# Token layers of a language-model tower: maxima by one transfer into 24 rows, parts split from PSUM, new order table

## The chip, the cores and the metric

One core of a Trainium2 chip runs the whole kernel: five engines (TensorE, VectorE or DVE, ScalarE or ACT, GpSimd or POOL, SyncE or SP) with queues of their own, and 16 DMA engines. The metric is the device time of one execution in microseconds (us).

## The reference, cut to what matters

The reference is a tower of five stages over 8 x 256 tokens of width 128: a four-layer transformer encoder (the *token layers*), a landmark attention mixer, a mixture of experts over frequencies, an attention with eight wide heads and a grouped attention chosen per sequence. The change touches the token layers alone:

```
x = embed[src] + _pos_encoding(s, D)
for i in range(N):                      # N = 4 layers, H = 8 heads of DK = 16
    q = (x @ Wq[i] + bq[i]).reshape(b, s, H, DK).transpose(0, 2, 1, 3)
    k = (x @ Wk[i] + bk[i]).reshape(b, s, H, DK).transpose(0, 2, 1, 3)
    v = (x @ Wv[i] + bv[i]).reshape(b, s, H, DK).transpose(0, 2, 1, 3)
    scores = jnp.einsum('bhqd,bhkd->bhqk', q, k) * scale        # scale = DK ** -0.5
    attn = jax.nn.softmax(scores, axis=-1)
    o = jnp.einsum('bhqk,bhkd->bhqd', attn, v)
    o = o.transpose(0, 2, 1, 3).reshape(b, s, D) @ Wo[i] + bo[i]
    x = _layernorm(x + o, g1[i], be1[i])
    f = jax.nn.relu(x @ W1[i] + b1[i]) @ W2[i] + b2[i]
    x = _layernorm(x + f, g2[i], be2[i])
return _layernorm(x, gf, bf)
```

Eight sequences of 256 tokens are held as four pairs (PAIRS = 4) of two sequences, b = 0 and b = 1. Everything is fp32 in the reference.

## The kernel before, in words

**Number format.** The score products run in bf16 with fp32 accuracy: q and k are each split into three bf16 parts that sum to the fp32 value. `packed` (one tensor for queries, side 0, and one for keys, side 1) holds per head 96 rows (MROW = 96): six stacked pairs of a query part and a key part, 16 features each. A matmul over 96 rows gives the fp32-like score.

**Softmax.** The scores are computed twice. First (steps M, `banks<-t_packed 96*128`, L2320) with queries in the rows of the result, from which DVE takes the negated row maximum (steps m, L2510). The maxima are split into three bf16 parts (Mp, L2518 to L2521), turned by TensorE to 24 rows (three parts by eight heads; MT, L2329), copied to SBUF by ACT (mt, L2436), stored to DRAM by a DMA on ACT's queue (ms, L2443) and loaded by another (ml, L2448) into the three rows 96 to 98 of side 0 of `packed`, one row per part, head by head. Side 1 holds ones in these three rows, filled once at the setup by ACT (L2739) and DVE (L2695). Then the scores are computed again with keys in the rows (steps S, 99 rows, L2341), the maximum already subtracted, ACT takes the exponential (E, L2455), and TensorE multiplies with v (AV, L2355).

**Splitting q and k.** A projection (Aq, Ak, L2308) leaves 128x512 in one of two PSUM banks, `lin`. ACT copies it with scale and bias to fp32 in SBUF (fq, fk, into `qf`) and once more to bf16 (pq, pk, first part). POOL subtracts (rq, rk, L2576), ACT rounds the remainder to bf16 (yq, yk, L2429), POOL subtracts again (zq, zk, L2582). SP stores the three parts to DRAM (sq, sk, L2251) and loads them again in three transfers each (lq, lk, L2257), which regroup them by head: 1.5 MB per pair. A load waits for the landing of its store (`keys_stored`, `parts_stored`).

**The other steps.** V and Vc (value projection), O, T1, TR, T2, t2 (the heads' result, transposed and divided), C1 (output projection), C1d, C1p, X1 (layer norm: sums and statistics on DVE, reciprocal root and normalisation, 3.1 us, on POOL, L2600), C2 and C2c (transpose), C3 and H (first feed-forward product and relu), C4 (second), C4d, C4p, X2 (norm), C5 and C5c (transpose into `xT` for the next layer), N1a to N2b (residual, POOL), W (SP loads the next layer's weights and waits for them), WP (POOL reorders the projection weights), RB (POOL adds the first output bias to the residual).

**What sets the order.** The table `PLACES` gives each step of each engine a time relative to its pair, and `PERIOD` the distance from pair to pair. `places_of` sorts step times plus PERIOD x pair for all 16 pair-layers; the sorted list is the instruction order of that engine. The times act through this order alone; semaphores do the rest. A step is issued only when all before it on its engine are. SP's queue runs stores, loads and W in order too. The 17 steps in LIN_STEPS take the two `lin` banks by turns in PE's order, and one may begin only when the step two before it in that list has been read out (`read_out`).

## Time and profile before

| what | value |
|---|---|
| median of 3 runs | 1250.07 us (1244.36 to 1254.27) |
| profiled execution, its own time | 1243.97 us |
| its span, first to last instruction | 1242.2 us |
| TensorE matmul busy | 1015.9 us, 82% |
| DVE, ACT, POOL busy | 688.1, 615.6, 418.2 us |
| mean granted TensorE clock | 0.902 of full |

The profiled execution's time and its span differ by 1.8 us of start and end. It lies 6.1 us under the median of the runs. The token layers run from 32.7 us (first projection) to 563.9 us (last residual); before that is the setup with the gather of the embeddings. In a timeline row the first number is the start, the second the busy time. Matmuls overlap their neighbours' ends, so the distance from one start to the next says what a step takes.

### The profile page before, as it was taken

To read this page: it belongs to the slowest core of one execution; us is meant where nothing else is said; L and a number is where in the kernel's file an instruction comes from. 1 tells how busy PE (TensorE), PEld (TensorE's weight loads), DVE (VectorE), ACT (ScalarE), POOL (GpSimd) and SP (SyncE) were. 2 spreads that over 40 slices of the span, in tenths; PEclk is the share of its full clock that TensorE was granted. 3 is DMA by queue.
4 is the path that set the end of the run, shared out by engine and by line. 5 is a ranking of instruction groups with operands and counts; after the bars stand their busy time and mean duration, and the time that the engine had idled before them with its cause. 6 is when DMAs were issued, how large, how long until landed. Compare 5 with 4: busy or idle time off the path is not lost. (4 is left out here: it accounts for less than half of the span.)

```text
span 1242.2 us, 20645 instructions
## 1 busy us (share of the span) xinstructions
PE 1015.9 (82%) x7048; PEld 706.4 (57%) x7048; DVE 688.1 (55%) x1957; ACT 615.6 (50%) x1369; POOL 418.2 (34%) x460
## 2 busy tenths in 40 slices
PE   1358999998999998852797999996999999834787
PEld 1124655555565555431486577785788888822453
DVE  4156766776777766126455111125577777857663
ACT  3235666665666665424534523325455555441455
POOL 5323656665676665457302000014300000031110
PEclk9678999998999999885698899997999999955789
DMA  7343644443343342002000011000000000008440
GB/s 89 76 104 71 148 97 92 103 95 78 79 119 79 90 92 54 3 1 69 1 1 1 19 34 35 23 25 1 18 10 10 19 27 1 2 13 141 78 89 28
DMA packets 52392, 65.70 MB, mean 53 GB/s; under 512 B 9629, under 2 KB 45881, under 8 KB 49209
## 3 DMA queue, kind: packets, MB, share of 16 engines
q1 hardware_dynamic: 49256, 62.35, 22.1%
q0 software_dynamic: 512, 1.05, 1.3%
q10 hardware_dynamic: 2520, 0.99, 0.4%
q8 instruction: 58, 0.95, 0.3%
q14 instruction: 46, 0.37, 0.1%
HBM read 47.09 MB, written 17.27 MB: 52 GB/s over the span
## 5 line engine op out<-in xcount | busy, mean ns | idle before, releaser
L2510 DVE TENSOR_REDUCE t_nmax<-banks 128x2 f32<-128x512 f32 x256 | 167.6, 687 | 66.6 <-PE banks L2320 63.5
L2455 ACT ACTIVATE t_probs<-banks 128x512 f32<-128x512 f32 x256 | 149.8, 593 | 69.4 <-PE banks L2341 65.5
L2341 PE MATMUL banks<-t_packed 99*128 99x256 bf16 x512 | 102.3, 284 | 21.9 <-DMA t_packed<-t_max_parts 21.2
L2320 PE MATMUL banks<-t_packed 96*128 96x256 bf16 x512 | 99.9, 280 | 23.6 <-DMA t_packed<-t_qk_pairs 20.5
L2600 POOL TENSOR_SCALAR xhat<-t_rbuf,mv,rstd 128x128 f32<-128x128 f32 x128 | 100.1, 795 | 3.3
L2320 PEld LDWEIGHTS banks<-t_packed 96*128 96x128 bf16 x512 | 45.9, 99 | 85.4 <-issue 52.2
L2341 PEld LDWEIGHTS banks<-t_packed 99*128 99x128 bf16 x512 | 44.5, 100 | 75.0 <-issue 35.8
L2355 PE MATMUL banks<-t_probs,t_v 128*32 128x256 f32 x1024 | 85.6, 403 | 0.1
L1548 ACT ACTIVATE hid<-banks,b 128x512 f32<-128x512 f32 x64 | 43.5, 686 | 69.5 <-PE banks L1453 68.8
L1872 ACT ACTIVATE l_probs<-banks,l_shift 128x256 f32<-128x256 f32 x128 | 59.5, 472 | 30.8 <-DVE l_shift L1911 28.1
L707 POOL TENSOR_TENSOR n_rstd<-n_vareps,mhalf 128x4 f32<-128x4 f32 x4 | 4.0, 1006 | 208.0 <-DVE n_nmean L690 207.9
L1591 DVE SCALAR_TENSOR_TENSOR acc<-banks,gates,acc 128x128 f32<-128x128 f32 (+1 forms) x72 | 20.1, 343 | 96.7 <-PE banks L1473 96.7
L2396 PE MATMUL banks<-x1T,wff 128*128 128x512 f32 x128 | 69.6, 633 | 0.9 <-ACT x1T L2474 0.9
L1473 PE MATMUL banks<-w,hid 128*128 128x128 f32 (+1 forms) x576 | 68.6, 280 | 1.1 <-DVE acc L1405 0.8
L1827 PE MATMUL banks<-vp,l_pT 128*128 128x128 f32 x512 | 67.9, 276 | 0.0
L1827 PEld LDWEIGHTS banks<-vp,l_pT 128*128 128x128 f32 x512 | 63.3, 192 | 6.2 <-issue 6.2
L1473 PEld LDWEIGHTS banks<-w,hid 128*128 128x128 f32 (+1 forms) x576 | 64.6, 184 | 3.6 <-DVE acc L1405 0.9
L1805 PE MATMUL banks<-xT,l_tq 128*128 128x256 f32 x256 | 65.9, 380 | 0.0
L2590 POOL TENSOR_SCALAR vareps<-mv 128x4 f32<-128x4 f32 x32 | 7.5, 234 | 166.4 <-DVE mv L2553 166.4
L2545 DVE TENSOR_TENSOR t_rbuf<-banks,R 128x512 f32<-128x512 f32 x32 | 22.1, 692 | 72.4 <-PE banks L2402 65.2
L2402 PE MATMUL banks<-wff,hidden 128*128 128x128 f32 x512 | 60.0, 275 | 0.8 <-ACT hidden L2481 0.8
L1453 PE MATMUL banks<-hT,w 128*128 128x512 f32 x128 | 59.8, 622 | 0.0
(364 smaller groups left out, 2305.1 us busy)
## 6 DMA issues: line engine op xcount, KB each, us to landing
t_qk_pairs<-t_parts SPq DMA_DIRECT2D x32, 384.0 KB, 2.5
t_packed<-t_qk_pairs SPq DMA_DIRECT2D x32, 384.0 KB, 6.3
t_packed<-t_qk_pairs SPq DMA_DIRECT2D x32, 256.0 KB, 6.0
g_packed<-g_qk_parts SPq DMA_DIRECT2D x48, 128.0 KB, 4.2
t_packed<-t_qk_pairs SPq DMA_DIRECT2D x32, 128.0 KB, 6.7
w<-in_L_ffn_w SPq DMA_DIRECT2D x16, 256.0 KB, 2.6
g_qk_parts<-g_parts SPq DMA_DIRECT2D x8, 384.0 KB, 4.9
wff<-in_L_tok_W SPq DMA_DIRECT2D x8, 256.0 KB, 7.7
```

Source lines behind the costliest of these rows:

```text
L1453: pe.matmul(banks[:, n % 4, :], w1[:, j, c * P:(c + 1) * P], hT[:, k * PW:(k + 1) * PW], start=True, stop=True).then_inc(sem["up_ready"], 1)
L1473: ins = pe.matmul(banks[0:rows, 4 + n % 2, k * P:(k + 1) * P], hid[:, j, c, i * P:i * P + rows], w2[:, j, c, :], start=(c == 0), stop=(c = ...
L1805: ins = pe.matmul(sc[:, n % 3, qt * S:(qt + 1) * S], tq[:, h % 2, c:c + P], m.xT[:, b * S:(b + 1) * S], start=True, stop=True)
L1827: ins = pe.matmul(av[:, n % 2, qt * D:(qt + 1) * D], pT[:, n % 2, kt, qt * P:(qt + 1) * P], vp[:, h % 2, 2 * b + kt, 0:D], start=(kt == 0) ...
L2320: ins = pe.matmul(m.mbank[:, n % 3, i * S:(i + 1) * S], m.packed[0:MROW, 0, p, h, c + qt * P:c + (qt + 1) * P], m.packed[0:MROW, 1, p, h, ...
L2341: ins = pe.matmul(m.sbank[:, n % 2, i * S:(i + 1) * S], m.packed[0:MROW + 3, 1, p, h, c + kt * P:c + (kt + 1) * P], m.packed[0:MROW + 3, 0 ...
L2355: ins = pe.matmul(m.obank[SLOT * i:SLOT * (i + 1), hq * S:(hq + 1) * S], m.v[:, 4 * p + 2 * b + kt, 4 * hq + i, :], m.probs[:, (n + i // 2 ...
L2396: filled(step, g, pe.matmul(bank, w.w1(l)[:, c * P:(c + 1) * P], m.x1T[:, g % 2, :], start=True, stop=True))
L2402: ins = pe.matmul(bank[:, i * P:(i + 1) * P], m.hidden[:, c, i * P:(i + 1) * P], w.w2(l)[:, c, :], start=(c == 0), stop=(c == 3))
L2455: act.activation(m.probs[:, n % 6, :], m.sbank[:, n % 2, :], ACT.Exp).then_inc(sem["probs_ready"], 1)
L2510: dve.tensor_reduce(m.nmax[:, b, u // 4, 2 * hp:2 * hp + 2], m.mbank[:, n % 3, :].rearrange("p (i k) -> p i k", i=2), AX.X, ALU.max, negat ...
L2600: ins = pool.tensor_scalar(m.xhat[:, k, i, :], m.rbuf[:, k, i, :], m.mv[:, k, i, 0:1], m.rstd[:, k, i:i + 1], ALU.subtract, ALU.mult)
```

## The change

A selector takes the place of the ones. Side 0 now holds all 24 rows of maxima (rows 96 to 119, TROW = 120) for every head, and side 1 holds for head h a one in the three rows of head h and zeros in the rest (`of_head`, built at the setup from the identity). So the 24 rows go from `mT` to `packed` in one transfer from SBUF to SBUF, each row written eight times, once per head. It is issued by SP (x0, x1). The score matmul S takes 120 rows.

```diff
+TROW = MROW + 3 * H
 # SP's queue
+                elif step in ("x0", "x1"):
+                    b = int(step[1])
+                    sp.wait_ge(sem["mrow_sb"], mrow_at[(b, g)] + 1)
+                    sp.dma_start(m.packed[MROW:TROW, 0, g % PAIRS, :, b * S:(b + 1) * S],
+                                 m.mT[0:3 * H, b, :].unsqueeze(1).broadcast_to([3 * H, H, S])).then_inc(sem["mrow"][b], 16)
 # TensorE, step S
-                                        m.packed[0:MROW + 3, 1, p, h, c + kt * P:c + (kt + 1) * P],
-                                        m.packed[0:MROW + 3, 0, p, h, c:c + S], start=True, stop=True)
+                        ins = pe.matmul(scores, m.packed[0:TROW, 1, p, h, c + kt * P:c + (kt + 1) * P],
+                                        m.packed[0:TROW, 0, p, h, c:c + S], start=True, stop=True)
 # ScalarE: fq, fk, ms0, ms1, ml0, ml1 are gone; pq and pk read the bank without a scale
-                elif step in ("ms0", "ms1"):
...
-                elif step in ("ml0", "ml1"):
...
+                    act.activation(m.parts[:, k, g % 2, 0 if k else 2], lin[turn[("Ak" if k else "Aq", g)][0]], ACT.Identity,
+                                   bias=w.qk_bias(l, k)).then_inc(sem["q_ready"], 1)
```

The remainder is taken by VectorE from the PSUM bank in one operation, and the factor DK ** -0.5 goes into the reordered weight:

```diff
 # VectorE
+                if step in ("rq", "rk"):
+                    k = 1 if step == "rk" else 0
+                    dve.wait_ge(sem["q_ready"], first_at[(k, g)] + 1)
+                    if g:
+                        dve.wait_ge(sem["split_done"], 2 * (g - 1) + k + 1)
+                    dve.scalar_tensor_tensor(out=rest[:, k], in0=lin[turn[("Ak" if k else "Aq", g)][0]], scalar=w.qk_bias(l, k),
+                                             in1=m.parts[:, k, g % 2, 0 if k else 2], op0=ALU.add, op1=ALU.subtract
+                                             ).then_inc(sem["rest_ready"], 1)
 # GpSimd
-                        pool.tensor_copy(w.qk_both(layer), w.proj_both(layer).rearrange("p c (h d) -> p c d h", h=H)
-                                         ).then_inc(sem["w_ordered"], 1)
-                elif step in ("rq", "rk"):
...
+                        pool.tensor_scalar(w.by_feature(layer, 0), w.by_head(layer, 0), DK ** -0.5, None, ALU.mult)
+                        pool.tensor_copy(w.by_feature(layer, 1), w.by_head(layer, 1)).then_inc(sem["w_ordered"], 1)
 # the setup: VectorE, then ScalarE
-            dve.memset(m.packed[MROW:MROW + 3, 1, 2:, :, :], 1.0)
+            dve.tensor_copy(m.identb[:, :], m.ident[:, :])
+            chain.step(dve.tensor_tensor(rows_of[:, :], m.ident[:, MROW:MROW + H], m.ident[:, MROW + H:MROW + 2 * H], ALU.add))
+            chain.step(dve.tensor_tensor(rows_of[:, :], rows_of[:, :], m.ident[:, MROW + 2 * H:TROW], ALU.add))
+            dve.tensor_copy(of_head[MROW:TROW, :, :], rows_of[MROW:TROW, :].unsqueeze(2).broadcast_to([3 * H, H, PW])
+                            ).then_inc(sem["rows_spread"], 1)
+            dve.wait_ge(sem["rows_spread"], 1)
+            for g in (0, 2):
+                dve.tensor_copy(m.packed[MROW:TROW, 1, g], of_head[MROW:TROW, :, :])
...
-            act.activation(m.packed[MROW:MROW + 3, 1, 0:2, :, :].rearrange("p a h n -> p (a h n)"),
-                           m.ident[MROW:MROW + 3, 0:1].broadcast_to([3, 2 * H * PW]), ACT.Copy, scale=0.0, bias=1.0)
+            act.wait_ge(sem["rows_spread"], 1)
+            for g in (1, 3):
+                act.activation(m.packed[MROW:TROW, 1, g], of_head[MROW:TROW, :, :], ACT.Copy)
```

The table is replaced: PERIOD goes from 25.065 to 26.69, and every step has a new time. What counts is the order that it gives. Sorted, one period repeats these lists, written from one Aq to the next; ' marks a step of the pair before, '' of the one before that, and so on.

```
before
PE      Aq S0.4'' AV0.0'' M0.3' Ak M0.4' S0.5'' M0.5' S0.6'' M0.6' V M0.7' S0.7'' AV0.1'' M1.0' C2''' S1.0'' M1.1' AV0.2'' S1.1'' C30''' M1.2' C31''' M1.3' MT0' S1.2'' M1.4' C32''' M1.5' C33''' S1.3'' M1.6' AV0.3'' M1.7' S1.4'' C4''' S1.5'' AV1.0'' S1.6'' AV1.1'' S1.7'' MT1' AV1.2'' S0.0' AV1.3'' T10'' S0.1' T11'' T20'' S0.2' M0.0 S0.3' T21'' M0.1 C5''' M0.2 C1''
ACT     ml1'' fq E0.4'' pq fk E0.5'' pk E0.6'' E0.7'' C2c''' yq E1.0'' H0''' yk H1''' mt0' E1.1'' ms0' H2''' E1.2'' H3''' E1.3'' O0'' ml0' E1.4'' E1.5'' E1.6'' E1.7'' mt1' ms1' O1'' E0.0' E0.1' t20'' E0.2' t21'' C5c''' E0.3'
DVE     C1d''' m0.3' m0.4' m0.5' m0.6' m0.7' Vc m1.0' Mp0' m1.1' m1.2' m1.3' m1.4' m1.5' m1.6' m1.7' Mp1' C4d''' TR0'' TR1'' m0.0 m0.1 m0.2
POOL    C1p''' X1''' rq rk zq zk N1a''' N2b'''' N1b''' C4p''' X2''' WP''' N2a'''
SP      sq sk lq lk W'''
after
PE      Aq AV0.1'' M0.3' Ak M0.4' S0.7'' M0.5' AV0.2'' M0.6' S1.0'' AV0.3'' S1.1'' M0.7' S1.2'' C2''' V M1.0' S1.3'' M1.1' C30''' S1.4'' M1.2' C31''' S1.5'' C32''' M1.3' C33''' MT0' M1.4' AV1.0'' M1.5' C4''' S1.6'' AV1.1'' S1.7'' M1.6' AV1.2'' T10'' AV1.3'' S0.0' M1.7' S0.1' T11'' T20'' S0.2' S0.3' T21'' AV0.0' S0.4' M0.0 C1'' C5''' S0.5' M0.1 S0.6' MT1' M0.2
ACT     mt1'' E0.5'' pq E0.6'' pk E0.7'' E1.0'' yq E1.1'' C2c''' yk E1.2'' E1.3'' H0''' O0'' H1''' H2''' H3''' E1.4'' mt0' E1.5'' E1.6'' E1.7'' O1'' E0.0' E0.1' t20'' E0.2' t21'' E0.3' E0.4' C5c'''
DVE     m0.1' m0.2' m0.3' rq m0.4' rk m0.5' m0.6' m0.7' Vc m1.0' Mp0' m1.1' m1.2' m1.3' m1.4' m1.5' C4d''' m1.6' TR0'' m1.7' TR1'' Mp1' m0.0 C1d''
POOL    C1p''' X1''' zq zk N1a''' N2a'''' N1b''' N2b'''' C4p''' X2''' WP'''
SP      x1'' sq sk lq lk x0' W'''
```

## Rows read from the trace of the kernel before

**Rows 1.** Timeline of TensorE: start, busy us, line, instruction [idle before <-releaser]
```profile
103.81 0.61 PE L2341 MATMUL banks<-t_packed 99*128 99x256 bf16 x2 [4.80 <-DMA t_packed<-t_max_parts]
...
110.48 1.02 PE L2308 MATMUL banks<-xT,wqk 128*128 128x512 f32 x2
...
451.41 1.10 PE L2308 MATMUL banks<-xT,wqk 128*128 128x512 f32 x2
```

**Rows 2.** Stretches Aq to Aq: length, PE, PEld, DVE, ACT, POOL busy, clock, DMA, GB/s
```profile
250.06:278.29 28.23, 26.41 (x214) 16.27 (x213) 20.07 (x50) 18.35 (x35) 18.92 (x21) 1.00 0.41 87
278.29:310.67 32.38, 28.86 (x215) 18.01 (x213) 20.10 (x50) 18.57 (x35) 18.32 (x20) 0.89 0.35 76
```

**Rows 3.** Waits of TensorE, 124 to 480 us: total, times, longest
```profile
PE banks L2341 <- DMA t_packed<-t_max_parts: 10.3, 8, 3.0
```

**Rows 4.** Timeline of TensorE in one period, and C4 of the period before
```profile
237.28 3.73 PE L2402 MATMUL banks<-wff,hidden 128*128 128x128 f32 x32
...
250.06 1.10 PE L2308 MATMUL banks<-xT,wqk 128*128 128x512 f32 x2
250.99 0.38 PE L2341 MATMUL banks<-t_packed 99*128 99x256 bf16 x2
251.30 0.64 PE L2355 MATMUL banks<-t_probs,t_v 128*32 128x256 f32 x8
251.87 0.39 PE L2320 MATMUL banks<-t_packed 96*128 96x256 bf16 x2
252.10 1.02 PE L2308 MATMUL banks<-xT,wqk 128*128 128x512 f32 x2
...
272.86 0.39 PE L2341 MATMUL banks<-t_packed 99*128 99x256 bf16 x2 [1.10 <-DMA t_packed<-t_max_parts]
...
276.73 0.60 PE L2390 MATMUL banks<-ident,xhat 128*128 128x128 f32 x4
...
277.39 1.06 PE L2382 MATMUL banks<-wproj,t_oT 128*128 128x128 f32 x8
278.29 1.10 PE L2308 MATMUL banks<-xT,wqk 128*128 128x512 f32 x2
```

**Rows 5.** SP's timeline, a stretch within the burst, SP's wait for weights
```profile
260.38 2.40 SPq L2251 DMA_DIRECT2D t_qk_pairs<-t_parts  x2
262.86 3.80 SPq L2257 DMA_DIRECT2D t_packed<-t_qk_pairs  x6
...
268.00:269.00 1.00, 1.00 (x11) 0.99 (x11) 0.00 (x0) 0.00 (x0) 0.00 (x0) 1.00 1.04 139
...
SPq L2273 <- DMA wff<-in_L_tok_W: 23.7, 3, 8.8
```

**Rows 6.** Timelines of ACT, its queue and POOL in the same period
```profile
258.36 0.62 ACT L2429 ACTIVATE t_parts<-rest 128x512 bf16<-128x512 f32 x1
265.07 0.71 ACTq L2448 DMA_DIRECT2D t_packed<-t_max_parts  x1
...
253.81 3.13 POOL L2600 TENSOR_SCALAR xhat<-t_rbuf,mv,rstd 128x128 f32<-128x128 f32 x4
256.90 2.28 POOL L2576 TENSOR_TENSOR rest<-t_qf,t_parts 128x512 f32<-128x512 f32 x2
261.23 1.16 POOL L2582 TENSOR_TENSOR t_parts<-rest,t_parts 128x512 bf16<-128x512 f32 x1 [0.93 <-ACT t_parts L2429]
```

**Rows 7.** Page, costliest groups: busy, mean ns, idle before
```profile
L2545 DVE TENSOR_TENSOR t_rbuf<-banks,R 128x512 f32<-128x512 f32 x32 | 22.1, 692 | 72.4 <-PE banks L2402 65.2
L2341 PE MATMUL banks<-t_packed 99*128 99x256 bf16 x512 | 102.3, 284 | 21.9 <-DMA t_packed<-t_max_parts 21.2
L2320 PE MATMUL banks<-t_packed 96*128 96x256 bf16 x512 | 99.9, 280 | 23.6 <-DMA t_packed<-t_qk_pairs 20.5
```

**Rows 8.** Timelines of DVE and POOL in the setup
```profile
7.78 6.88 DVE L2695 MEMSET t_packed<- 3x8192 bf16 x1 [1.75 <-issue]
...
9.22 0.94 POOL L2711 DMA_INDIRECT R<-in_L_tok_embed,ids  x1 [0.30 <-issue]
```

More of the change, by code:

```diff
@@ L2204, in token_layers @@
     for step, g in order["pe"]:
-        key = (step, g)
-        if key[0] in LIN_STEPS:
-            turn[key] = (n % 2, n // 2)
+        if step in LIN_STEPS:
+            turn[(step, g)] = (n % 2, n // 2)
             n += 1
@@ L2215, in token_layers @@
     root_at = {(x[0][0:2], x[1]): i for i, x in enumerate(rooted)}
-    rest_at = {(int(x[0] == "rk"), x[1]): i for i, x in enumerate(y for y in order["gpsimd"] if y[0] in ("rq", "rk"))}
+    rest_at = {(int(x[0] == "rk"), x[1]): i for i, x in enumerate(y for y in order["vector"] if y[0] in ("rq", "rk"))}
+    first_at = {(int(x[0] == "pk"), x[1]): i for i, x in enumerate(y for y in order["scalar"] if y[0] in ("pq", "pk"))}
+    mrow_at = {(int(x[0][2]), x[1]): i for i, x in enumerate(y for y in order["scalar"] if y[0] in ("mt0", "mt1"))}
     second_at = {(int(x[0] == "yk"), x[1]): i for i, x in enumerate(y for y in order["scalar"] if y[0] in ("yq", "yk"))}
@@ L2234, in read_out @@
         if step in ("Aq", "Ak"):
-            return sem["q_ready"], 4 * g + (2 if step == "Aq" else 4)
+            return sem["rest_ready"], rest_at[(int(step == "Ak"), g)] + 1
         if step[0:2] in ("MT", "T1", "T2"):
-            name = {"MT": "mrow_sb", "T1": "otok_ready", "T2": "oT_ready"}[step[0:2]]
+            if step[0] == "M":
+                return sem["mrow_sb"], mrow_at[(int(step[2]), g)] + 1
+            name = {"T1": "otok_ready", "T2": "oT_ready"}[step[0:2]]
             return sem[name], 2 * g + int(step[2]) + 1
@@ L2409, in _ @@
                 l, p = layer_of(g), g % PAIRS
-                if step in ("fq", "pq", "fk", "pk"):
-                    k = 1 if step[1] == "k" else 0
+                if step in ("pq", "pk"):
+                    k = 1 if step == "pk" else 0
                     lin_ready(act, "Ak" if k else "Aq", g)
-                    if step[0] == "f":
-                        out = m.qf[:, k, g % 2]
-                        if g >= 2:
-                            act.wait_ge(sem["split_done"], 2 * (g - 2) + k + 1)
-                    else:
-                        out = m.parts[:, k, g % 2, 0 if k else 2]
-                        if g >= 2:
-                            act.wait_ge(sem["keys_stored"] if k else sem["parts_stored"], 16 * (g - 1))
-                    act.activation(out, lin[turn[("Ak" if k else "Aq", g)][0]], ACT.Identity,
-                                   bias=w.qk_bias(l, k), scale=1.0 if k else DK ** -0.5
-                                   ).then_inc(sem["q_ready"], 1)
+                    if g >= 2:
+                        act.wait_ge(sem["keys_stored"] if k else sem["parts_stored"], 16 * (g - 1))
+                    act.activation(m.parts[:, k, g % 2, 0 if k else 2], lin[turn[("Ak" if k else "Aq", g)][0]], ACT.Identity,
+                                   bias=w.qk_bias(l, k)).then_inc(sem["q_ready"], 1)
                 elif step in ("yq", "yk"):
@@ L2494, in _ @@
                 l, p = layer_of(g), g % PAIRS
-                if step == "Vc":
+                if step in ("rq", "rk"):
[6 more added lines that the diff above has]
+                                             ).then_inc(sem["rest_ready"], 1)
+                elif step == "Vc":
                     if new_layer(g):
@@ L2641, in tok_transformer @@
     qk_cols, qk_bias = sb("qk_cols", [P, LAYERS, 2]), sb("qk_bias", [P, LAYERS, 2])
+    of_head, rows_of = sb("of_head", [P, H, PW], BF16), sb("rows_of", [P, H])
     ids, idf = sb("ids", [P, TILES], I32), sb("idf", [P, 2, TILES])
```

40 lines of the change are left out of this document (11 added, 29 removed), and 40 rows, old and new, of the table PLACES.

## The prediction, made before the kernel was changed

> **What bounds the kernel now.** I read the page first (TensorE is busy 82% of the span, the clock is mostly full), then a table of stretches from one pair's first projection (step Aq) to the next pair's, then TensorE's waits, then the timelines of one such period on each engine. The token layers are 16 pair-periods. Aq of pair 3 starts at 110.48 us and Aq of pair 15 at 451.41 [rows 1], so twelve periods take 340.93 us, 28.41 each. In a quiet one TensorE is busy 26.41 of 28.23 us at full clock [rows 2]: TensorE is near its limit, but 1.8 us per period is something else. The list of waits names it: the score step S0.0 waits for the transfer of the maxima, eight times, 10.3 us [rows 3]. The timeline shows why, and it is a loop, not a short transfer. Aq starts at 250.06, the first load of the packed parts is issued at 262.86, which is 12.80 later [rows 4, 5]; all 16 DMA engines then work at a share of 1 or more, and S0.0 is released at 272.86, 10.00 after that first load; the next Aq starts at 278.29, 5.43 later [rows 4, 5]. 12.80 + 10.00 + 5.43 = 28.23, the whole period. The maxima's small load was issued at 265.07 [rows 6], so it needed 7.8 us beside that burst. So the period is the time from Aq to the burst, the burst, and the way from S0.0 to the next Aq. Why is the burst late? The remainder (step rq, POOL) waits for POOL's normalisation, 253.81 to 256.94, then two remainders take 2.28, then come ACT's second part and POOL's third, 1.16 [rows 6].
>
> **The change, part by part.** Every step is counted from the start of Aq of the same period; T means that moment.
>
> Split from PSUM. Removed per pair: two ACT copies (fq, fk) and two POOL subtractions; added: two DVE operations from one PSUM and one SBUF operand, 128x512. The nearest row of that form is the residual sum, 692 ns [rows 7]. DVE is busy 20.07 of 28.23 us [rows 2], so 1.4 more is hidden in its idle time; if DVE had none, it would cost 1.4 per period. POOL's 2.28 us of subtraction leave the path.
>
> Where the burst starts. In the new PE order, S1.0 stands after Aq, Ak, two AV, four M and one S. From start to start, Aq takes 0.93, AV 0.57, M 0.23 and an S with the hand-off behind it 0.31 [rows 4]; with 0.87 for Ak this is 0.93 + 0.87 + 1.14 + 0.92 + 0.31, about 4.15 us after T. ACT's order has yq behind E1.0, so E1.0 (0.6) ends near T + 5.1, yq (0.62, [rows 6]) near 5.75, POOL's zq (1.16) near 6.95. POOL is free for it: C1 stands before C5, two M, two S and MT1, so it ends about 1.5 us earlier than before (C5 and one M alone are 0.66, 276.73 to 277.39, [rows 4]), and POOL's normalisation ends near T + 5.4 instead of 6.88. From the store to the first load is 2.48 [rows 5]: the first load leaves at T + 9.5, with hand-offs 9.7, instead of 12.8.
>
> The maxima's transfer. Two DMAs on ACT's queue, 12 KB each, become one on SP's, 96 KB, SBUF to SBUF; it is read eight times. Its cost alone is nowhere in the trace: the nearest row is the store of parts, four times its bytes, 2.48 us to the first load [rows 5]; the upper end is the 7.8 us beside the burst. For b = 1 nothing else is in flight and I take 2.5; for b = 0 it is issued (after H3, E1.4 and mt0) near T + 14.2, behind all six loads on the same queue, and I take the end of the burst plus 0.6: 9.7 + 10.0 + 0.6 = T + 20.3. The new order wants S0.0 at about the same time: from S1.0 to MT0 come one AV, C2 (as C5, 0.44), V (as C1, 0.90), four C3 (0.87 each) and 11 M or S (0.23), 7.9 us; from there to S0.0 four AV, C4 (3.73 busy from 237.28, some 3.6 to the next step), T10 (0.44), MT0 (0.2) and five M or S, 7.7 us, with hand-offs 8: T + 20 [rows 4]. From S0.0 to the next Aq the new order has six score steps, not three: 18 steps, with AV 0.57, C1 0.90, C5 0.44, T11 0.5 and about 0.22 for the others, 6.1 us. The loop is then 20.3 + 6.1 = 26.4.
>
> The queue rule speaks against this. The small load went out on ACT's queue while SP's burst ran, and still took 7.8 us [rows 4, 6]. The Trainium skill, DMA: Bandwidth & Descriptors, section Queues, rings and completion order, says that every DMA engine takes turns between the queues, a packet at a time, and takes one queue's descriptors in order; by that rule the old place let the maxima slip in between and the new one puts them last. By that rule S0.0 would have been served early before, the gain would be only the waits' own time, and the sum would be the third rival's; the row shows that taking turns bought next to nothing.
>
> The period. The loop gives 26.4, TensorE's own work 26.4 to 26.5 [rows 2]. Two equal limits never mesh, so I take 26.8. 12 x (28.41 - 26.8) = **-19.3 us**. This mean includes the one bad period of 32.38 us at clock 0.89, where a 3 us wait let the clock fall to its 1.2 GHz level [rows 2]; against the quiet periods alone it would be 12 x 1.4 = -17.
>
> The fill. The first bursts gate in the same way: S0.0 of pair 1 waits 4.80 until 103.81, and Aq 3 follows at 110.48 [rows 1]. Two bursts before Aq 3 start about 3.1 us earlier each, 6.2, but the way from S0.0 to Aq has more score steps, each at ACT's pace of 0.6 while nothing else is there, some 1.3 us each time, 2.6: between -1 and -6, **-3.6**.
>
> 120 rows instead of 99 in the score matmul. 96 rows cost 280 ns and 99 cost 284 [rows 7], the same 256 columns; I take 0. If the 4 ns were the price of three rows, 21 more would be 28 ns, 512 times, 14 us; but more of the S steps lie in the stretch at half clock, and that explains 4 ns.
>
> Setup. Two fills of one engine each (DVE 6.88 us, ACT) go; DVE gets one spreading copy of 24x4096 and two bf16 copies, ACT two. DVE's would end near 20 us and are needed by nobody before 29: hidden under the gathers. But the gathers' descriptors are made by POOL, and they are the path of the setup. The old 8192-element fill ran beside the gathers, which kept their 0.94 us each [rows 8], which gives 0 as one end; three copies of 4096 at its rate are 10.3 us, the other end if POOL stood still meanwhile. I take **+1**, near the fill. The Trainium skill, SBUF — State Buffer, section Who interferes with whom, says that copies and casts of DVE in a two-port mode hold a port pair that POOL needs, for the whole instruction. By that rule the setup would grow by most of DVE's copy time; no row of this trace has a large DVE copy, so none bears it out.
>
> Queues. SP waits for the last weight load, up to 8.8 us [rows 5], and the transfer x1 of the pair before now stands behind it. The weights are issued near T + 15 to 17, so SP is free near T + 26 and x1 is wanted at T + 27.2: hidden, 1 us to spare, three times. POOL's weight reordering is two operations, not one, some 0.5 us in POOL's idle time. The issue of the old DMAs leaves ACT's queue.
>
> The tail. MT1 stands behind S0.6, and the last pair has no M steps or projections to cover x1: 0 to +3, **+1**, since another wait (for xhat) partly holds the same time.
>
> Sum: -19.3 - 3.6 + 1 + 1 = -20.9, from the profiled execution's own 1243.97 us: 1223. That execution lies 6 us under the median of the runs, 1250.07, near their lowest; a new median may lie as far up, so I say **1226 us** half-way.
>
> **The rivals.**
>
> Slower: the burst is not earlier. If yq, behind E1.0, S1.0 and x1 in ACT's order, keeps the first load at T + 12.8, then x0 lands at 12.8 + 10.0 + 0.6 = 23.4, and with 6.1 the period is 29.5: 12 x 1.1 = +13; a 3 us stall per period lets the clock fall as at 300 us, which cost about 2 us more there, so up to +24. 1257 to 1268, say 1262. It decides from T + 11.7 on (11.7 + 10.6 + 6.1 = 28.4). Against it: POOL's subtractions are gone. Chance 0.14.
>
> No change: x1 is slow. Its cover between MT1 and S1.0 is about 4.5 us: C5c and mt1 on ACT, then 2.5 of transfer need 3.7. If the transfer takes 5 us, S1.0 and with it yq and the burst move by 1.7, the period is near 28.1, and only the fill and the bad period gain: 1241. For it: its 192 pieces are unlike any row. Chance 0.2.
>
> Only the named waits go: the loop is a coincidence of this trace, the period falls by the waits' 10.3 us over twelve, and the fill gives 3.6: -12, with setup and tail 1232. Chance 0.14.
>
> The change doesn't do what it says: the transfer moves the same maxima and its eightfold read has no effect that anyone waits for; this falls together with the forecast or the second rival and gets no chance of its own.
>
> **How the numbers follow.** Forecast (1212 to 1235) 0.5, the three rivals 0.48, anything else 0.02. Range **1207 to 1256**: the lower end is a period of 26.5 and the fill's 6; the upper end takes in the second rival and a setup of +10. A difference of 1%, 12.5 us, is about what a measurement of this kernel tells from none. Under 1237.6: the forecast and the third rival, 0.64 with their tails; within: the second rival and the lower part of the first, 0.23; slower than 1262.6: 0.13.
>
> **What would show it.** The period (Aq to Aq) at 26.8; the first load under 10 us after Aq; S0.0 released within 1 us of the end of the burst and waiting under 1 us; xhat no longer in TensorE's waits, since C2 stands later than POOL's normalisation; the gathers' spacing unchanged beside DVE's copies; the score matmul's mean still near 280 ns. I am wrong if S1.0 waits for x1, if the first load stays at 12 us or more after Aq, or if the period falls and a new wait on another step takes it back.

## The result, and the profile after

The changed kernel takes 1240.52 us (median of 20 runs, 1235.47 to 1246.13), the kernel before 1247.24 (20 runs beside them). The ratio is 0.9933, interval 0.9913 to 0.9953: a real gain, but 0.7%, where 2% was forecast. The value lies in the range, the gain at a third of what the working gave.

In the profiled executions the last residual of the token layers ends at 555.7 us instead of 563.9: 8.1 us less. The rest of the kernel, which the change does not touch, took 7.2 us more in this one execution, partly at a lower clock (0.70 against 0.80 in the stretch from 36 to 76 us behind the token layers), so its span is 1241.2. The medians of the runs differ by 6.7, near the 8.1 of the token layers; that the 7.2 us behind them are scatter is taken from this, not shown by a second profile.

TensorE's timeline of one quiet period, from Aq to Aq (start, busy us, line, instruction [idle before <-releaser]), as [rows 4]:

```profile
308.67 1.02 PE L2314 MATMUL banks<-xT,wqk 128*128 128x512 f32 x2
...
330.17 0.39 PE L2348 MATMUL banks<-t_packed 120*128 120x256 bf16 x2 [1.23 <-DMA t_packed<-t_mT]
...
336.23 1.02 PE L2314 MATMUL banks<-xT,wqk 128*128 128x512 f32 x2
```

SP's queue in the same period, as [rows 5]:

```profile
315.71 2.33 SPq L2252 DMA_DIRECT2D t_qk_pairs<-t_parts  x2
318.49 2.99 SPq L2258 DMA_DIRECT2D t_packed<-t_qk_pairs  x6
322.36 14.93 SPq L2282 DMA_DIRECT2D t_packed<-t_mT  x2
```

The first load now leaves 9.82 us after Aq (318.49 less 308.67) instead of 12.80. But S0.0 is released 11.68 after it, not 10.00, and the next Aq follows 6.06 later. Three stretches of the same kind as [rows 2] (length, PE, PEld, DVE, ACT, POOL busy, clock, DMA share, GB/s):

```profile
110.21:138.53 28.32, 26.23 (x214) 16.15 (x213) 20.82 (x56) 17.50 (x33) 15.12 (x19) 1.00 0.57 135
138.53:168.58 30.05, 27.57 (x214) 17.37 (x213) 20.80 (x53) 17.72 (x33) 16.55 (x19) 0.94 0.42 87
308.67:336.23 27.56, 26.12 (x215) 16.20 (x213) 20.83 (x53) 17.52 (x33) 16.09 (x18) 1.00 0.43 94
```

The last has 1.44 us in which TensorE does nothing, nearly all before S0.0. The second is 2.5 us longer. Of this, 1.2 is the clock: behind a wait of 2.24 us before S0.0 its mean is 0.76 in the stretch to the next Aq (161.35 to 168.58), so it was at its 1.2 GHz level for a part of it, and the stretch takes 7.23 us instead of 6.06. The other 1.3 are a first load that left 0.8 later and a release 0.5 later. Aq of pair 3 starts at 110.21 and Aq of pair 15 at 447.29, so twelve periods take 337.08 us, 28.09 each (before 28.41).

TensorE's waits from 124 to 480 us (line, releaser: total us, times, longest), all rows, as [rows 3]:

```profile
PE banks L2348 <- DMA t_packed<-t_mT: 19.8, 13, 2.2
PE banks L2380 <- DVE t_otok L2525: 2.3, 11, 0.2
PE banks L2326 <- DVE t_nmax L2505: 1.0, 2, 0.7
```

The kernel before had, in the same window, next to the wait of [rows 3]:

```profile
PE banks L2390 <- POOL xhat L2600: 6.8, 14, 0.5
PE banks L2320 <- DMA t_packed<-t_qk_pairs: 2.6, 3, 0.9
```

The waits for xhat and for the packed parts are gone. The wait that the change meant to shorten is the one that grew: thirteen times, 19.8 us in all, where it was eight times, 10.3 us.

The group of the score matmul on the page, as [rows 7] (count | busy, mean ns):

```profile
L2348 PE MATMUL banks<-t_packed 120*128 120x256 bf16 x512 | 100.7, 285 | 34.9 <-DMA t_packed<-t_mT 34.1
```

120 rows take 285 ns on the mean where 99 took 284: 21 more rows cost nothing that shows here.

### The profile page after: what moved, and what is told of

The parts are those of the page before. It is cut to its first block and busy times, and to the rows that moved or that the text cites. A ratio compares the mean times of both kernels' runs of the same rounds, so it can differ in the third digit from the quotient of the medians.

```text
span 1241.2 us, 20532 instructions
## 1 busy us (share of the span) xinstructions
PE 1016.0 (82%) x7048; PEld 711.3 (57%) x7048; DVE 696.7 (56%) x1993; ACT 601.7 (48%) x1338; POOL 386.8 (31%) x432
## 5 line engine op out<-in xcount | busy, mean ns | idle before, releaser
L2348 PE MATMUL banks<-t_packed 120*128 120x256 bf16 x512 | 100.7, 285 | 34.9 <-DMA t_packed<-t_mT 34.1
L2348 PEld LDWEIGHTS banks<-t_packed 120*128 120x128 bf16 x512 | 44.5, 100 | 90.2 <-DMA t_packed<-t_mT 41.7
L2408 PEld LDWEIGHTS banks<-wff,hidden 128*128 128x128 f32 x512 | 58.4, 192 | 2.5 <-ACT hidden L2468 2.3
```

Of the source, the lines that this page charges most:

```text
L2348: ins = pe.matmul(scores, m.packed[0:TROW, 1, p, h, c + kt * P:c + (kt + 1) * P], m.packed[0:TROW, 0, p, h, c:c + S], start=True, stop=True)
L2408: ins = pe.matmul(bank[:, i * P:(i + 1) * P], m.hidden[:, c, i * P:(i + 1) * P], w.w2(l)[:, c, :], start=(c == 0), stop=(c == 3))
```

## The experiments

The question is where the gain went. **Theory 1**: x0 is late because it stands behind the whole burst on SP's queue. **Rivals**: its bytes or pieces cost the time, whatever queue; or the wait is only where slack shows, and another limit holds the period at 27.5. For each kernel "release" is the time from the first load of the burst to S0.0, and "period" the mean of the twelve from Aq of pair 3 to Aq of pair 15. The ratios are to the kernel before, measured again beside each group of runs; the changed kernel's own is 0.9933 (0.9913 to 0.9953).

**e1: x0 and x1 on ACT's queue.**

```diff
-# SP's table      ("x0", 41.28), ("x1", 53.91)
+# ACT's table     ("mt0", 40.79), ("x0", 40.80), ... ("mt1", 53.42), ("x1", 53.43)
...
-                    sp.dma_start(m.packed[MROW:TROW, ...
+                    act.dma_start(m.packed[MROW:TROW, ...
```

> The changed kernel, with the two transfers of the maxima (96 KB each) issued on ACT's queue, right behind the copy that they read, instead of SP's. Theory 1 (place in the queue): on SP's queue x0's data comes last, behind all six loads of the burst, so S0.0 is released 12.15 us after the first load; on a queue of its own it is let in between and S0.0 is released 10.3 to 10.7 us after the first load. Its wait (1.5 us per period) goes, the period falls from 28.09 to 26.7, the time to about 1224, ratio to the kernel before 0.981. Rival (bytes): the engines are full, and the eightfold read has to be carried wherever it is queued; release stays 11.8 to 12.2 after the first load, the period 28.0, the time 1240, ratio 0.993. Second rival: ACT's queue pays for the issue (some 0.1 us twice) and the loads of the burst end later by what x0 takes out of it: M steps of the next pair wait, period 27.5.

Measured: 1239.35 us, ratio 0.997 (0.9939 to 1.0001), period 28.09, the same as in the changed kernel. In the last six periods the release is 11.5 to 12.5 after the first load, 11.85 on the mean; on SP's queue it is 11.7 to 12.4, mean 12.05. The time doesn't differ either: the interval takes in the changed kernel's ratio. Which packets move when is seen in windows of a microsecond on the DMA queues. ACT's transfer is issued here:

```profile
323.78 0.79 ACTq L2435 DMA_DIRECT2D t_packed<-t_mT  x1
```

The packets of the queues (q1 is SP's, q10 ACT's: packets, MB, share of 16 engines) from 328 to 329, then from 329 to 330 us:

```profile
q1 hardware_dynamic: 30, 0.17, 78.9%
```

```profile
q10 hardware_dynamic: 125, 0.06, 48.3%
q1 hardware_dynamic: 32, 0.07, 37.1%
```

Not one packet of ACT's queue moves in the 5.2 us between the issue and 329; then 192 of its 204 move by 330.5, at the very end of the burst (125 in the window shown, 67 in the half microsecond behind it). So a queue of its own did not let the transfer pass what had been issued before it.

**e2: one head instead of eight, from the second layer on.**

```diff
-                    sp.dma_start(m.packed[MROW:TROW, 0, g % PAIRS, :, b * S:(b + 1) * S], ... [3 * H, H, S]
+                    hs = H if g < PAIRS else 1
+                    sp.dma_start(m.packed[MROW:TROW, 0, g % PAIRS, 0:hs, b * S:(b + 1) * S], ... [3 * H, hs, S]
```

> The changed kernel, but from the second layer on the two transfers write the rows of one head only (12 KB each instead of 96 KB); the other heads keep the maxima of the first layer. Bytes theory: the last stretch of the burst, near 1 us at about 100 GB/s, goes, S0.0 is released about 1 us earlier (11.1 after the first load) and the twelve periods fall by 0.8 to 1.0 us each where the wait was: time 1230, ratio 0.985. Place theory: the data is little either way, only the fixed way of a transfer that starts behind the burst counts: release at 11.9 to 12.2 after the first load, time 1239, ratio 0.993.

Measured: 1233.06 us, ratio 0.9924 (0.9895 to 0.9954), period 27.45; in the last six periods the release is 11.1 to 11.6, mean 11.40. In the trace the eightfold read is worth 0.65 us of release and as much of the period: two fifths of the 1.67 that the period lies above its floor (e3), not all. The ratios of the two kernels alone could not tell them apart; their intervals overlap.

**e3: no transfer from the second layer on.**

```diff
+                elif step in ("x0", "x1") and g >= PAIRS:
+                    pass
...
-                        pe.wait_ge(sem["mrow"][b], 16 * (g + 1))
+                        pe.wait_ge(sem["mrow"][b], 16 * min(g + 1, PAIRS))
```

> The changed kernel, but from the second layer on no maxima are moved at all and the score steps don't wait for them (stale maxima are used): what the whole loop through the transfer costs. Loop theory: without this wait the next limit is TensorE's own work, 26.1 to 26.4 us of a period; the twelve periods from the fourth pair on fall from 28.09 to 26.5 each, the time to 1221, ratio 0.979. Rival (the wait is only where the slack shows): another wait (packed parts of the next pair, ACT's exponentials, DVE's maxima) takes its place and the period stays at 27.5 or more: time above 1233, ratio 0.989 or more.

Measured: 1222.9 us, ratio 0.9828 (0.981 to 0.9846). Once the layers without the transfer run, every period is 26.42 or 26.43. One of them:

```profile
301.16:327.58 26.42, 26.24 (x214) 16.14 (x213) 21.36 (x53) 17.38 (x33) 16.11 (x18) 1.00 0.41 91
```

TensorE is busy 26.24 of 26.42 us. This settles two points: the floor of the prediction, 26.4 to 26.5, was right, and nothing but this one wait stands above it. The burst without x0 can be read here too. The slices (same columns) from 8 to 10 us after the first load, and of the changed kernel from 9 to 12 after its own:

```profile
318.97:319.97 1.00, 1.00 (x16) 0.47 (x12) 0.97 (x5) 0.70 (x2) 0.00 (x0) 1.00 0.96 213
319.97:320.97 1.00, 1.00 (x16) 0.58 (x12) 0.93 (x6) 0.14 (x1) 0.38 (x2) 1.00 0.20 41
```

```profile
327.49:328.49 1.00, 1.00 (x16) 0.58 (x12) 0.93 (x6) 0.14 (x1) 0.39 (x2) 1.00 0.65 96
328.49:329.49 1.00, 0.45 (x8) 0.00 (x0) 0.75 (x3) 0.48 (x1) 0.90 (x2) 1.00 0.26 38
329.49:330.49 1.00, 0.32 (x3) 0.30 (x4) 0.00 (x0) 0.11 (x1) 1.00 (x2) 1.00 0.02 5
```

Without x0 the mean share adds up to 9.2 us in this period, which is one of the shortest: the last large packet of the burst ends 9.8 us after the first load here, 9.8 to 10.8 in the ten such periods, 10.4 on the mean. With x0 the engines work on at a falling share, moving its small pieces, and single pieces are late: from 329.49 to the start of S0.0 at 330.17 the changed kernel's queue still has

```profile
q1 hardware_dynamic: 10, 0.00, 2.3%
```

The last of them ends at 329.7, 0.5 us before S0.0. In the trace's own packet times x0's first piece moves 9.0 us after the first load in this period, the last ends at 11.2, and S0.0 starts at 11.68. On the mean of twelve periods these are 9.4, 11.5 and 12.15: x0 waits for what is ahead of it, then takes 2.0 us for its own pieces, and 0.7 pass until S0.0. With one head (e2) they are 9.3, 10.3 and 11.6: the pieces take 1.1 us less, but 1.3 and not 0.7 pass behind the last one. Why, no run here shows.

**e4: half a burst from the second layer on** (one load of three per operand).

```diff
...
-                for row, part, parts in ((0, 0, 3), (3, 0 if k else 1, 2), (5, 0 if k else 2, 1)):
+                for row, part, parts in (...)[0:3 if g < PAIRS else 1]:
```

> The changed kernel, but from the second layer on only the first of the three loads of each operand is made (384 KB instead of 768 KB; the other rows stay as the first layer left them), everything else the same: half of the burst. Loop theory (Aq to the first load 9.7, burst 10.9 and release 1.2, S0.0 to Aq 6.2): the burst falls by 4 to 5 us, S0.0 is no longer gated by it, and the period falls to the same floor as without the transfer, 26.5: time 1221, ratio 0.979. Rival: x0 by itself (96 KB, eightfold read) takes long whatever stands before it, and S0.0 keeps waiting; period 27.5 or more, ratio 0.989 or more.

Measured: 1221.71 us, ratio 0.9829 (0.9811 to 0.9847), periods of 26.42 to 26.43 from the third of the twelve on. With the transfer of 96 KB in place and 768 KB fewer before it, S0.0 waits for it once between 124 and 480 us, 1.8 us. The transfer is late because of what is before it. The tail of the changed kernel says the same: x1 issued at 500.0 with nothing else in flight released S1.0 at 502.65, 2.6 us later; the prediction took 2.5.

**e5: x0 between the queries' and the keys' loads.** If only the loads issued before x0 delay it, three are enough to put behind it, and nothing need be left out.

```diff
-        ("sq", 7.36), ("sk", 9.4), ("lq", 10.48), ("lk", 12.52), ("x0", 41.28), ("x1", 53.91), ("W", 97.43),),
+        ("sq", 7.36), ("sk", 9.4), ("lq", 10.48), ("lk", 14.7), ("x0", 41.28), ("x1", 53.91), ("W", 97.43),),
```

One number: lk of a pair sorts at 41.39 in the time of the pair before, so behind x0 at 41.28.

> The changed kernel with one move in SP's order: the transfer x0 of the pair before stands between the three loads of the queries and the three loads of the keys, instead of behind all six. The six loads alone end 9.2 us after the first, and the data of x0 then takes 1.4 and its landing 1.1 more. Theory (x0 is late only because the packets ahead of it are the whole burst): with 768 KB of the 1536 ahead of it, x0 lands at 4.6 + 1.4 + 1.2 = 7 to 8 us after the first load, before S0.0 asks for it at 10.6; the wait at S0.0 goes, the burst ends 1.4 later and is still 2 us ahead of M0.0; the period falls to the floor of the kernel without transfers, 26.4 to 26.5, the time to 1223, ratio to the kernel before 0.982. Rival: the keys' loads come too late and M0.0 waits for the packed parts by 1 us or more: period 27.5, ratio 0.989 or more. Second rival: the eightfold read is slow beside the rest wherever it stands and S0.0 goes on waiting over 1 us: ratio 0.993.

Measured: **1209.99 us** (6 runs), ratio 0.9673 (0.9636 to 0.971). The best kernel of the study, 30 us under the changed one. SP's queue and one period:

```profile
295.37 1.27 SPq L2258 DMA_DIRECT2D t_packed<-t_qk_pairs  x3
299.23 0.82 SPq L2282 DMA_DIRECT2D t_packed<-t_mT  x1
300.10 1.45 SPq L2258 DMA_DIRECT2D t_packed<-t_qk_pairs  x3
```

```profile
285.54:311.97 26.43, 26.25 (x214) 16.15 (x213) 21.39 (x53) 17.40 (x33) 16.14 (x18) 1.00 0.46 98
```

x0 is issued 3.86 us after the first load, exactly as late as in the changed kernel (322.36 less 318.49 is 3.87); but its small pieces move between 300.7 and 302.0, 5.3 to 6.6 after the first load, where there they moved at 9.0 to 11.2. SP keeps the keys' loads back until x0 is out (from 296.64 to 300.10), the engines have the queries' loads to move meanwhile, and no M step waits for the keys. From 124 to 480 us one wait for a transfer of maxima is left, 1.2 us at 471.78, in the tail. It beats e3's time because the fill gains as well: Aq of pair 3 starts at 100.11 instead of 110.21, ten of the 30 us, which e3 cannot show since it changes nothing in the first layer.

**e6: e5, and the selector spread by ACT alone.**

```diff
-            dve.tensor_copy(of_head[MROW:TROW, :, :], rows_of ...
-            for g in (0, 2):
-                dve.tensor_copy(m.packed[MROW:TROW, 1, g], of_head[MROW:TROW, :, :])
+            # ScalarE
+            for g in range(PAIRS):
+                act.activation(m.packed[MROW:TROW, 1, g], rows_of[MROW:TROW, :].unsqueeze(2).broadcast_to([3 * H, H, PW]), ACT.Copy)
```

> The kernel of e5 and, in the setup, the selector's rows spread by ACT alone, four times from the small table, without the three DVE copies. In the changed kernel two of POOL's gathers took 3.36 and 1.53 us instead of 0.94 while DVE's copies ran, and the first projection began 1.5 us later than before. Theory (DVE's copies hold POOL up): all gathers at 0.94 to 1.3, first projection at 32.6 to 33.0 instead of 34.2, 1.3 us off the time of e5. Rival (the gathers were slow for another reason, such as the loads of the weights): the two long gathers stay and the first projection stays at 34. Second rival: ACT's four spreads of 4 us each end after 27 and hold up the biases: first projection at 34 or later.

The setup of the changed kernel, DVE and then POOL:

```profile
6.37 2.29 DVE L2689 CAST of_head<-rows_of 24x4096 bf16<-24x4096 f32 x1
8.70 2.37 DVE L2693 COPY t_packed<-of_head 24x4096 bf16<-24x4096 bf16 x2
```

```profile
6.68 3.36 POOL L2706 DMA_INDIRECT R<-in_L_tok_embed,ids  x1 [0.30 <-issue]
10.35 1.53 POOL L2706 DMA_INDIRECT R<-in_L_tok_embed,ids  x1 [0.30 <-issue]
```

The next gather takes 0.94 again. And e6, where DVE does nothing in these microseconds:

```profile
6.58 0.95 POOL L2701 DMA_INDIRECT R<-in_L_tok_embed,ids  x1 [0.30 <-issue]
...
10.33 0.95 POOL L2701 DMA_INDIRECT R<-in_L_tok_embed,ids  x1 [0.30 <-issue]
```

The two gathers are back at 0.95: DVE's copies did hold POOL up, by 2.4 and 0.6 us. The first projection comes at 31.64 instead of 34.12. But the time is 1210.2, ratio 0.968 (0.9632 to 0.9728), as without it: Aq of pair 3 is at 100.46 (e5: 100.11). The fill took the 2.5 us back; what in it did is open.

**e7: the old split in the new order** (fq, fk before pq, pk on ACT; rq, rk on POOL before zq; the rest of the changed kernel).

> The changed kernel with the old split alone put back: two more copies on ACT per pair (fq, fk) and the remainders on POOL, not DVE, in the new order. Theory (the loop runs through the split): the first load leaves 1 to 1.6 us later after Aq (fq's 0.69 and POOL's 1.14 against DVE's 0.74, hand-off the same), so S0.0 is released that much later and the period rises from 28.1 to 29.2 or more: time 1253, ratio to the kernel before 1.004. Rival (the split lies in slack, the gain came from the order of the steps): first load within 0.3 us of 9.7 after Aq, ratio 0.993.

Measured: 1260.3 us, ratio 1.0086 (1.006 to 1.0112), period 29.59. The first load leaves 11.1 to 11.6 us after Aq (328.42 less 317.30 is 11.12) instead of 9.7. POOL holds it up:

```profile
319.43 3.14 POOL L2593 TENSOR_SCALAR xhat<-t_rbuf,mv,rstd 128x128 f32<-128x128 f32 x4
322.54 2.28 POOL L2569 TENSOR_TENSOR rest<-t_qf,t_parts 128x512 f32<-128x512 f32 x2
324.77 1.16 POOL L2575 TENSOR_TENSOR t_parts<-rest,t_parts 128x512 bf16<-128x512 f32 x1
```

The first step of the prediction is confirmed: the normalisation and POOL's subtractions were the way to the burst. The period grows by the 1.5 us of the delay, but not by that alone: the release is 0.4 shorter, 11.8 on the mean, and in six of the twelve periods S0.0 to Aq takes 7.2 instead of 6.06, as it does in the changed kernel behind a fallen clock.

**e8: the old transfer in the new order** (ms0, ml0, ms1, ml1 on ACT at their old distances, 99 rows, old setup; the new split).

> The changed kernel with the old way of the maxima put back alone (store of 12 KB to the chip's memory and load of 12 KB into three rows, both on ACT's queue; 99 rows in the score step, old setup), in the new order. Theory (two hops against one, both behind the same burst): the store issued near the middle of the burst needs 2 us or more, the load behind it waits for the packets already queued and lands with the end of the burst, 9.2 + 1.2 = 10.4 to 11 after the first load, since it is 24 pieces and not 192: S0.0 waits less than in the changed kernel, period 27.0 to 27.5, and setup 1.5 us shorter: time 1231, ratio 0.985; then the new transfer cost 0.7 us per period. Rival: the second hop starts only after the first has crossed the burst, so it lands at 12.5 or later and the period is 28.5 or more: ratio 0.998 or more; then the new transfer gained.

Measured: 1303.93 us, ratio 1.0433 (1.0382 to 1.0485), period 32.94. The rival is right, and the place of the cost is ACT: what TensorE waits for most is now ACT's exponentials, in the AV steps (124 to 480 us: total, times, longest):

```profile
PE banks L2361 <- ACT t_probs L2454: 35.4, 11, 4.3
```

ACT's queue issues the store at 325.80, and when ACT comes to the load behind it, it stands until the store has landed:

```profile
325.80 0.30 ACTq L2442 DMA_DIRECT2D t_max_parts<-t_mT  x1
329.57 0.60 ACT L2454 ACTIVATE t_probs<-banks 128x512 f32<-128x512 f32 x1 [3.33 <-PE banks L2348]
333.51 0.71 ACTq L2447 DMA_DIRECT2D t_packed<-t_max_parts  x1
334.33 0.60 ACT L2454 ACTIVATE t_probs<-banks 128x512 f32<-128x512 f32 x1 [4.16 <-DMA t_max_parts<-t_mT]
```

12 KB need 7.7 us: in the new order the burst has been issued 4.2 us before. In the old order the store went out at 261.94, before the first load at 262.86, and its load 3.13 us later.

**e9: the kernel before with the new split alone; e10: with the new transfer alone, behind all six loads; e11: e10 with x0 between the queries' and the keys' loads.** Old order of the other steps in all three.

```diff
 # e9, old table
+# DVE      ("rq", 195.0), ("rk", 196.5), ("Vc", 196.87)        fq, fk gone from ACT
 # e10, old table
+# SP       ("lq", 203.74), ("lk", 205.21), ("x0", 230.5), ("x1", 236.03), ("W", 282.39)
 # e11
+# SP       ... ("x0", 229.5) ...        lk of the next pair sorts at 230.275
```

> The kernel before with the new split alone (first part on ACT, remainder on DVE from PSUM); the old order of the steps and the old way of the maxima stay. Theory (the loop Aq to the first load, burst, S0.0 to Aq): putting the old split into the changed kernel made the first load 1.5 us later (11.2 after Aq for 9.7) and the period 1.5 longer, so here the first load should come at 11.3 after Aq instead of 12.8, and the period fall from 28.4 to 26.9: time 1229, ratio 0.985. Rival (in the old order the first load hangs on something else, POOL's normalisation, which takes until 6.9 us after Aq): first load at 12.3 or later, period 28.0, ratio 0.996 or more.

Measured: 1267.26 us, ratio 1.0146 (1.009 to 1.0203), period 29.81. The first load does not come earlier, it comes at 14.12 us after Aq (303.98 less 289.86): 12.3 or later, as the rival had it, but not by the rival's cause, since POOL is done with its normalisation 6.9 us after Aq as before and then stands idle. TensorE's waits from 124 to 480:

```profile
PE banks L2314 <- DVE rest L2502: 15.0, 12, 1.3
PE banks L2351 <- DMA t_packed<-t_max_parts: 13.4, 11, 1.9
PE banks L2399 <- DVE rest L2502: 5.0, 12, 0.4
```

A bank of a projection is now free only when DVE has taken the remainder, and in the old order V and C2 stand too close behind. With C2 late, ACT's copy of it is late (298.83, 8.97 after Aq, where it was 7.63), and yq stands behind that copy in ACT's order: 299.51, 9.65 after Aq, instead of 8.3 [rows 4, 6].

> The kernel before with the new transfer alone (96 KB on SP's queue, behind all six loads), the old order of the other steps and the old split. Theory: the first load stays 12.8 us after Aq, the release comes 12.1 after it instead of 10.0, with 5.4 to the next Aq a period of 30.3: time 1271, ratio 1.018. Rival (the old order had the maxima ready earlier, so what matters is only that one hop is less): period 28.4 or less, ratio 1.000 or less.

Measured: 1302.83 us, ratio 1.045 (1.0398 to 1.0503), period 32.43. The sign and the mechanism hold, the size was short by half: first load 12.8, release 12.5 on the mean, and 6.5 to 7.8 from S0.0 to Aq instead of the 5.4 reckoned, behind waits of 3 to 4 us.

> The same kernel as e10, except that x0 stands between the queries' and the keys' loads: old order of the other steps, old split, new transfer with 768 KB of the burst behind it. Theory (the place of the transfer among the loads is what decides, the split and the order of the steps are worth little once S0.0 is not gated): the period falls to TensorE's own work, 26.4 to 26.6, time 1218 to 1224, ratio 0.979. Rival (the late burst, 12.8 us after Aq, and the keys' loads behind x0 now gate M0.0, or POOL's normalisation gates C2): a new wait of 1 us or more per period on the packed parts or on xhat, period 27.4 or more, ratio 0.990 or more.

Measured: 1239.27 us, ratio 0.9937 (0.9904 to 0.9969), period 27.90. S0.0 no longer waits (0.6 us in all), and two others do:

```profile
PE banks L2399 <- POOL xhat L2596: 8.4, 14, 1.8
PE banks L2329 <- DMA t_packed<-t_qk_pairs: 6.4, 9, 1.4
```

The rival is right, in both of its parts: with the burst 12.8 us after Aq, the place of x0 is paid for by the M steps, which wait for the packed parts 6.4 us in all, and C2 waits 8.4 us for POOL's normalisation. In e5, with the early burst and the new order, no M step waits for packed parts.

**e12: ACT's queue and one head together.** The edits of e1 and e2.

> The changed kernel with the transfers on ACT's queue (as in e1) and, from the second layer on, of one head only (12 KB, 24 pieces; the other heads keep older maxima). On ACT's queue the 192 pieces of e1 did not begin before 5 us after the issue, and S0.0 was released 11.6 after the first load; the kernel before, with 24 pieces on ACT's queue, was released at 10.0. Theory (a transfer waits for the 8 KB packets that the engines hold already, then takes turns with the rest, so few pieces pass and many do not): release at 10.2 to 10.6 after the first load, period 26.6 to 26.9, ratio 0.982 to 0.985. Rival (place and number change nothing together that they did not apart): release at 11.2 to 11.4 as with one head on SP's queue, ratio 0.992.

Measured: 1235.18 us, ratio 0.9884 (0.9833 to 0.9934), release 11.2 to 12.1, mean 11.56 in the last six periods, period 27.71. Few pieces on a queue of their own did not pass either; the theory is out. ACT's issue and the queues' packets from 325 to 326 us; until 325 ACT's queue has none:

```profile
320.39 0.74 ACTq L2436 DMA_DIRECT2D t_packed<-t_mT  x1
```

```profile
q1 hardware_dynamic: 46, 0.22, 103.4%
q10 hardware_dynamic: 4, 0.00, 1.3%
```

## Why the prediction was wrong

**The step that failed** is the maxima's transfer for b = 0: "the end of the burst plus 0.6: 9.7 + 10.0 + 0.6 = T + 20.3". From the first load to S0.0 it has 10.6; measured are 12.15. The three terms of the loop, each the mean of twelve periods (us):

| from | forecast | before | changed |
|---|---|---|---|
| Aq to the first load | 9.7 | 12.92 | 9.69 |
| first load to S0.0 | 10.6 | 9.63 | 12.15 |
| S0.0 to the next Aq | 6.1 | 5.86 | 6.25 |
| sum | 26.4, taken as 26.8 | 28.41 | 28.09 |

The first term gained 3.2 us, as forecast. The second gave 2.5 of them back. Over twelve periods that leaves -3.85 us instead of -19.3. Two readings went into the 10.6, and both were wrong.

First, 10.00 was taken as the length of the burst. It was the release of a small transfer inside it. The packets of the kernel before, from 270.8 to 271.4 us and from 271.4 to 274.5, 7.9 to 8.5 and 8.5 to 11.6 us after the first load:

```profile
q1 hardware_dynamic: 27, 0.11, 126.2%
q10 hardware_dynamic: 27, 0.01, 18.8%
```

```profile
q1 hardware_dynamic: 67, 0.28, 48.3%
```

All 24 pieces of the maxima moved in the first window, and 0.28 MB of the burst came behind them. That the burst ends near 10 all the same (10.4 in e3) is luck. What x0 costs behind it is 1.8 us, not 0.6.

Second, the 7.8 us from issue to release were taken for the rest of the burst. They are what a transfer needs behind that which was issued before it: 7.8 before, 7.8 for x0 in the period shown (322.36 to 330.17), 7.75 on ACT's queue (e1), 7.6 there with one head (e12); over the twelve periods of the changed kernel it is 7.5 to 9.1, mean 8.1. But ml0 was issued 2.2 us after the first load, while SP was still issuing its loads, and x0 3.9 us after it, with all six out. The change brought the burst 3.1 us forward and the maxima only 1.3 (15.0 to 13.7 us after Aq), so more of it lay ahead of them. The prediction held both numbers that it needed: issue at T + 14.2 and 7.8 to the release give T + 22.0, with 6.1 a period of 28.1, which is what was measured. It set the 7.8 aside as an upper end.

In ten periods S0.0 to Aq takes 6.06. In two it takes 7.23, at a mean clock of 0.76, behind waits of 2.24 and 1.80 us; waits of 1.84 and 1.88 us left the clock at 1.00, so the length of a wait alone did not decide it. The periods with the two are 30.05 and 29.30, the other ten average 27.8.

**The queue rule.** The Trainium skill (DMA: Bandwidth & Descriptors, section Queues, rings and completion order) has the engines take turns between queues a packet at a time. Counted in the profile's packets of 8 KB, this would have let e1 and e12 pass, and their rows show that it did not: no packet of ACT's queue in e1 for 5.2 us, 4 in e12 until 326. But the same section counts typically 9 to 17 descriptors to a packet. The burst's 1536 KB are 192 of the profile's packets, by an estimate twelve for each of 16 engines; if each is one descriptor, an engine's whole share may be a single packet of the rule, and the rows don't refute it. The prediction was right not to count on taking turns, but drew the wrong price from that: not "a transfer waits for the end of the burst anyhow" but "it waits for what is issued before it". The consequence that it named, that the old place let the maxima in between and the new one puts them last, came true.

**The other steps.** The first load at T + 9.7: right, and for the reason given (e7). TensorE's floor 26.4 to 26.5: right, 26.42 (e3). S0.0 to Aq 6.1: right as a number, but the prices listed for its 18 steps add up to 5.5, so nothing written there leads to 6.1. 120 rows at no cost: right. x1 at 2.5 us, never waited for before the tail: right. xhat out of the waits: right. Fill: -1.74 net of the setup against -3.6; S0.0 of pair 1 still waits 4.97 there, and e5 shows what this wait and that of pair 0 were worth, ten us. The tail was mis-signed: from Aq of pair 15 to the last residual 108.4 us against 112.5, -4, where +1 was forecast. Setup: +1.5 against +1, and by the mechanism that I had set aside. The gathers beside DVE's copies took 3.36 and 1.53 us instead of 0.94, and without the copies 0.95 (e6). The Trainium skill's rule (SBUF — State Buffer, section Who interferes with whom) agrees; it was the small size of the copies (4.7 us in all, not the 10.3 of my bound) that kept my number near, which is luck. The lower end of the range doesn't follow from its terms either: a period of 26.5 and a fill of 6 give 1215, not 1207.

Sum of the profiled executions: setup +1.5, fill -1.7, twelve periods -3.9, tail -4.0, -8.1 together.

**The rivals.** "No change: x1 is slow" gave 1241 and the time is 1240.5, but its mechanism is refuted: x1 took 2.6 us and no step waited for it. "Only the named waits go" is refuted as well: the named wait grew. "Slower: the burst is not earlier" did not happen, but e7 and e9 show what a late burst costs: first load at 11.1 and 14.1 us, 0.9 and 1.5% slower than before. No rival had the burst early and the maxima late, which is what happened; x0's issue should have been reckoned against the first load, and not only against Aq.

**Parts.** No part of the change gains alone: split alone +1.5%, transfer alone +4.5%, all but the split +0.9%, all but the transfer +4.3%. Only together do they come to -0.7%, and with x0 in front of the keys' loads to -3.3%. With that place alone the new transfer gives -0.6% in the old order and with the old split (e11), as much as the whole change within the intervals. The new order with neither the new transfer nor the new split was not run, nor e5 with the old split, so how the remaining 2.7% divide between order and split is open.

## What to carry to other kernels

When a small transfer is waited for beside a burst, count what has been issued before it on any queue: moving it ahead of half of the burst was worth 30 us here, an eighth of its pieces 0.65 us of a period of 28.1, a queue of its own nothing that could be told from scatter. A time from issue to landing that was read beside a burst is added to the issue, not to the end of the burst. A change that brings a burst forward must bring forward what the next step needs from the same engines by as much. And an order table, a transfer and a split that were made for each other can't be judged part by part: hold the sum against the engine's floor (26.42 us here) and name the one wait that stands between.

## What the runs showed of the hardware that was not expected

- A transfer of 12 or 96 KB issued into a running burst of large packets (e1: 137 packets with 0.74 MB from 324 to 328 us) released its matmul 7 to 9 us after its issue in nearly all periods, on SP's queue or ACT's, in 24 pieces or 192; the extremes within the twelve periods are 6.9 in e2 and 9.8 in e12. With nothing in flight it took 2.6.
- From the end of x0's last piece to the matmul that waited for it 0.4 to 1.0 us passed in the changed kernel, 0.7 on the mean.
- TensorE's granted clock fell behind waits of 2.24 and 1.80 us (0.76 on the mean of the 7.23 us that follow) and not behind waits of 1.84 and 1.88 (1.00). In e7 it fell behind one of 1.66 and not behind one of 2.30.
- A DVE copy of 24x4096 (1.2 to 2.3 us) beside an indirect DMA that POOL was making lengthened that one from 0.94 to as much as 3.36 us; a DVE fill of 6.88 us had not [rows 8].
- ACT spread 24x4096 in 3.5 us each (14.12 for four, e6), DVE in 2.29 from fp32 and 1.18 from bf16. With ACT the first projection came 2.5 us earlier, though the end time didn't show it.
